# A graph layer with residual and layer norm: another warm-up operand, eight banks for the weight preparation, and its transposes put into two groups

## The chip, the cores and the metric

The kernel runs on one core of a Trainium2 chip. The metric is the device time of one execution in microseconds. PE is TensorE (PEld its weight loads), DVE is VectorE, ACT is ScalarE, POOL is GpSimd, SP is SyncE. PSUM has eight banks of 128 partitions by 512 fp32 columns; PE writes its results there.

## The reference

The input is x (32 batches, 256 nodes, 512 features), an adjacency of 256 by 256, four weights of 512 by 512 and two scalars. Cut to what matters:

```python
z_l = h @ W_lang.T;  z_g = h @ W_grav.T;  v = h @ W_V.T
zn  = z_l / max(norm(z_l), EPS)
A_l = max(zn @ zn.T, 0) * not_eye
d2  = max(sq + sq.T - 2 * z_g @ z_g.T, 0)
A_g = exp(-d2 / (2 * sigma**2)) * not_eye
K   = w_l * row_stochastic(A_l * adj) + (1 - w_l) * row_stochastic(A_g * adj)
x   = layernorm(x + (K @ v) @ W_O.T)
```

## The kernel before

Every fp32 matrix is split into a high and a low part in PE's rounded fp32 format, and a product is the sum of three (high by high, high by low, low by high).

**Preparation.** Before the first batch the kernel works out the two symmetric matrices M = W.T W of W_lang (called L) and W_grav (called G), and the product of W_V and W_O. The work is a list, `prep_units`, of 22 units, run by PE in the order of the list. Each unit fills one PSUM bank, and ACT and then DVE copy it out as its high and its low part:

- UPPER (g, i): one row of blocks of M, 12 products. For i = 0 they are 512 columns wide, for i = 1 to 3 they are 256 wide (the function `row_blocks`; the other blocks of the row come by symmetry).
- MIRROR (g, i): two transposes of 128 by 128 out of `m_hi`, the blocks that symmetry gives; ACT alone copies them out and counts them in `mirrored`. They read the rows that `made(r, i)` names.
- WO_TURN (i): four transposes of W_O, which lies in the tile `y`.
- WVO (i): 12 products of 512 columns, W_V by the turned W_O. The first waits until POOL has made the low part of W_V (`v_split`) and DVE that of the last WO_TURN.

The order before is UPPER L 0 to 3, UPPER G 0, then for i = 1, 2, 3: MIRROR L i, WO_TURN i-1 (with WO_TURN 3 in the last round), UPPER G i; then MIRROR G 1, WVO 0, MIRROR G 2, WVO 1, MIRROR G 3, WVO 2, WVO 3. Unit u goes to bank u % 4 and waits (`emptied`) until unit u - 4 has been copied out. Each MIRROR waits for ACT's copy of the last UPPER row of its matrix (`prepared(UPPER, g, DT - 1)`).

ACT runs `prep_hi_part(u)` and DVE `prep_lo_part(u)` in the order of the units. Between them stand other pieces of work at fixed units: on ACT the casts of W_V (`value_weight_hi`) and, at the units `SPLIT_AT` (WVO 0 and WVO 1), the high parts of the first two batches (`turn_hi`); on DVE their 32 by 32 block transposes (`turn`), their low parts (`turn_lo`), the `diagonals`, `scales` and `scaled_rest` of M. POOL makes the low part of W_V, then the triangles that give `md_hi`, ending in `m_ready[g]`.

**Before the preparation** PE runs `WARM` = 9 products of zeros. DVE clears a tile of 512 columns (`kt_hi` of batch 0) for them. PE then needs `ident_ready`, which POOL gives, and then starts with UPPER L 0 (`first_block`), whose parts it waits for one 128-row block at a time (`w_hi_ready`, `w_lo_ready`).

**The body.** Batches are taken in 16 pairs: pairs 0, 1 and 14 are written out, twelve are in a hardware loop, and the last has an order of its own. A pair has eight projections (`project`, four for L and then four for G), four tiles of values, four tiles of x M x.T, and the four products K by v of the pair before. Projection k goes to bank (22 + k) % 4; in pair 0 the first four wait with `emptied(PREP - 4 + k)`, later ones for `proj_ready`. Banks 4 and 5 take the x tiles, banks 6 and 7 the products with v.

## Time and profile before

| | |
|---|---|
| Time, median of 3 runs | 650.01 us (648.86 to 652.34) |
| Time of the profiled execution | 648.58 us |
| Its span in the trace | 646.8 us |
| PE busy | 638.5 us, 2861 products and transposes |
| DVE, ACT, POOL busy | 534.9, 384.1, 136.5 us |

A busy time is the sum over one engine's instructions. Products are pipelined, so the printed length of one is longer than the distance to the next: what a product costs in a stream is the distance from one start to the next. Times in rows count from the start of the span.

### The profile page before, as it was taken

To read this page: it belongs to the slowest core of one execution; us is meant where nothing else is said; L and a number is where in the kernel's file an instruction comes from. 1 tells how busy PE (TensorE), PEld (TensorE's weight loads), DVE (VectorE), ACT (ScalarE), POOL (GpSimd) and SP (SyncE) were. 2 spreads that over 40 slices of the span, in tenths; PEclk is the share of its full clock that TensorE was granted. 3 is DMA by queue.
4 is the path that set the end of the run, shared out by engine and by line. 5 is a ranking of instruction groups with operands and counts; after the bars stand their busy time and mean duration, and the time that the engine had idled before them with its cause. 6 is when DMAs were issued, how large, how long until landed. Compare 5 with 4: busy or idle time off the path is not lost.

```text
span 646.8 us, 10734 instructions
## 1 busy us (share of the span) xinstructions
PE 638.5 (99%) x2861; PEld 529.2 (82%) x2861; DVE 534.9 (83%) x1431; ACT 384.1 (59%) x709; POOL 136.5 (21%) x287
## 2 busy tenths in 40 slices
PE   9999999999999999999999999999999999999996
PEld 7888888888888888888888888888888888888884
DVE  6874979798897978889797988879788887978786
ACT  5544545656565565656556575655657565565775
POOL 3612011211221121122112112221211222121132
PEclk9999999999999999999999999999999999999999
DMA  9321757483765748385574938657492865546353
GB/s 299 80 62 61 187 142 165 133 244 96 216 161 171 199 128 249 94 245 143 160 198 138 250 83 242 148 163 193 141 250 79 253 141 161 160 151 192 100 184 123
DMA packets 141509, 106.48 MB, mean 165 GB/s; under 512 B 40112, under 2 KB 115632, under 8 KB 141488
## 3 DMA queue, kind: packets, MB, share of 16 engines
q1 hardware_dynamic: 140768, 104.40, 57.9%
q0 software_dynamic: 288, 1.05, 0.5%
q10 hardware_dynamic: 432, 0.79, 0.3%
q8 instruction: 9, 0.15, 0.1%
q14 instruction: 12, 0.10, 0.0%
HBM read 65.80 MB, written 40.40 MB: 164 GB/s over the span
## 4 chain that ended last, share of the span: by engine, by line
PE 98%; ACT 0%; DVE 0%; issue 0%; POOL 0%; POOLq 0%
PE bank L1425 62%; PE bank L1515 18%; PE bank L1520 15%; PE bank L1472 2%; PE bank L1493 1%; PE bank L1561 0%; PE bank L1482 0%; PE bank L1477 0%; ACT y L821 0%; PE bank L1448 0%; PE bank L1451 0%; PE bank L1452 0%; POOL last_rstd L680 0%; DVE xq L1322 0%; DVE m_lo L1316 0%
## 5 line engine op out<-in xcount | busy, mean ns | idle before, releaser
L761 ACT ACTIVATE p_hi<-bank,m_scale 128x512 fp32r<-128x512 f32 x128 | 86.2, 684 | 54.9 <-PE bank L1520 53.8
L1061 DVE SCALAR_TENSOR_TENSOR p_lo<-bank,m_scale,p_hi 128x512 fp32r<-128x512 f32 x128 | 94.2, 747 | 19.0 <-ACT p_hi L761 18.9
L1520 PE MATMUL bank<-hT_lo,m_hi 128*128 128x512 f32 x384 | 107.8, 389 | 0.0
L1425 PE MATMUL bank<-wvo_hi,hT_hi 128*128 128x512 f32 x256 | 99.8, 390 | 0.0
L1425 PE MATMUL bank<-wvo_hi,hT_lo 128*128 128x512 f32 x256 | 99.6, 389 | 0.0
L1425 PE MATMUL bank<-wvo_lo,hT_hi 128*128 128x512 f32 x256 | 99.6, 389 | 0.0
L1425 PE MATMUL bank<-p_hi,hT_hi 128*128 128x512 f32 x256 | 99.6, 389 | 0.0
L1425 PE MATMUL bank<-p_lo,hT_hi 128*128 128x512 f32 x256 | 99.6, 389 | 0.0
L1520 PEld LDWEIGHTS bank<-hT_lo,m_hi 128*128 128x128 f32 x384 | 72.1, 188 | 15.0
L628 POOL TENSOR_TENSOR rnorm<-norm,minus_half 128x2 f32<-128x2 f32 x32 | 34.8, 1088 | 231.0 <-DVE norm L1089 231.0
L1515 PE MATMUL bank<-hT_hi,m_lo 128*128 128x512 f32 x192 | 69.5, 389 | 0.0
L765 ACT CAST v_hi<-bank 128x512 fp32r<-128x512 f32 x60 | 32.4, 589 | 62.5 <-PE bank L1425 62.5
L776 ACT COPY xs<-bank 128x512 f32<-128x512 f32 x64 | 37.2, 581 | 47.2 <-PE bank L1425 47.2
L1515 PE MATMUL bank<-hT_hi,m_hi 128*128 128x512 f32 x192 | 64.3, 389 | 0.0
L1425 PEld LDWEIGHTS bank<-wvo_hi,hT_lo 128*128 128x128 f32 x256 | 48.0, 188 | 10.0
L1425 PEld LDWEIGHTS bank<-p_lo,hT_hi 128*128 128x128 f32 x256 | 48.1, 188 | 10.0
L1425 PEld LDWEIGHTS bank<-p_hi,hT_hi 128*128 128x128 f32 x256 | 48.0, 188 | 10.0
L1425 PEld LDWEIGHTS bank<-wvo_lo,hT_hi 128*128 128x128 f32 x256 | 48.1, 188 | 9.9
L1425 PEld LDWEIGHTS bank<-wvo_hi,hT_hi 128*128 128x128 f32 x256 | 48.0, 188 | 9.9
L1515 PE MATMUL bank<-hT_hi,md_hi 128*128 128x512 f32 x128 | 49.8, 389 | 0.0
L1176 DVE SCALAR_TENSOR_TENSOR work<-work,coef 128x256 f32<-128x256 f32 x60 | 26.5, 483 | 25.6 <-ACT work L795 25.6
L1425 PE MATMUL bank<-v_hi,kt_hi 128*128 128x512 f32 x120 | 46.9, 391 | 0.0
(164 smaller groups left out, 1266.7 us busy)
## 6 DMA issues: line engine op xcount, KB each, us to landing
x_blk<-in_x SPq DMA_DIRECT2D x128, 128.0 KB, 3.4
x_spill<-xs SPq DMA_DIRECT2D x30, 512.0 KB, 3.8
xq<-x_spill SPq DMA_DIRECT2D x120, 128.0 KB, 3.4
x_nat<-in_x SPq DMA_DIRECT2D x30, 512.0 KB, 4.0
out_y<-y SPq DMA_DIRECT2D x30, 512.0 KB, 3.4
k_spill<-work SPq DMA_DIRECT2D x30, 256.0 KB, 2.2
work<-k_spill SPq DMA_DIRECT2D x120, 64.0 KB, 2.2
r_row<-r_spill SPq DMA_DIRECT2D x32, 128.0 KB, 3.5
```

Of the source, the lines that this page charges most:

```text
L628: nc.gpsimd.tensor_tensor(rnorm[:, b, 0:NT], norm2[:, b], minus_half[:], ALU.pow).then_inc(pool_steps, 1)
L761: nc.scalar.activation(p_hi[:, :, j, g, :], src[:].rearrange("p (b n) -> p b n", b=2), ACT.Copy, scale=m_scale[:, g, j:j + 1]).then_inc(pr ...
L765: nc.scalar.copy(last_v(m_hi, b, t) if is_last(p) else v_hi[:, b, t], src[:]).then_inc(proj_hi, 1)
L776: nc.scalar.copy(dst, src).then_inc(x_saved, 1)
L1061: nc.vector.scalar_tensor_tensor(out=p_lo[:, :, j, g, :], in0=src[:].rearrange("p (b n) -> p b n", b=2), scalar=m_scale[:, g, j:j + 1], in ...
L1176: nc.vector.scalar_tensor_tensor(out=wk_row(b, KER, t), in0=wk_row(b, KER, t), scalar=coef[:, b, L, t:t + 1], in1=wk_row(b, GAUSS, t), op0 ...
L1425: last = pe.matmul(dst, lhsT, rhs, start=(n == 0), stop=(n == len(steps) - 1))
L1472: last = pe.matmul(row_blocks(dst[:], i), lhsT, rhs, start=(n == 0), stop=(n == len(steps) - 1))
L1493: pe.matmul(kv_bank[1][:], kt_hi[:, 0, 0, 0], in_kt(kt_hi, 0), start=True, stop=True)
L1515: pe.matmul(pbank(k)[:], stationary, hi[i], start=(i == 0), stop=False)
L1520: last = pe.matmul(pbank(k)[:], md_hi[:, g, 0] if i == 0 else m_hi[:, g, i, c], lo[i], start=False, stop=(i == DT - 1))
```

## The change

Three things are edited.

- The zeros for the first products: POOL clears 128 columns of `kt_hi` as its first instruction, ahead of `ident`, where DVE cleared 512 columns. Each product reads the 128 columns four times as its moving operand (a pattern with stride 0), and is still 512 columns wide. There are eight products in place of nine.
- The banks: unit u goes to bank u % 8 and waits for unit u - 8. The first four projections wait for the last unit that used their bank (`last_unit_in`).
- The order: MIRROR L 1 to 3 and WO_TURN 0 to 3 stand together behind UPPER G 0; UPPER G 1 to 3 and WVO 0 follow; MIRROR G 3, 1, 2 stand together behind WVO 0; WVO 1 to 3 end the list. A MIRROR waits for the rows that it reads and no longer for the last row. The first projection of each matrix waits for the latest of its mirrors (`mirrors_of`).

```diff
--- before.py
+++ after.py
@@ -230,6 +230,7 @@
 
 
         bank = [ctx.enter_context(nc.psum_tensor(f"bank{i}", [P, WIDE], F32)) for i in range(8)]
+        prep_bank = bank
         proj_bank = bank[0:4]
         x_bank = bank[4:6]
         kv_bank = bank[6:8]
@@ -329,15 +330,11 @@
 
         UPPER, MIRROR, WO_TURN, WVO = range(4)
 
+
         prep_units = [(UPPER, L, i) for i in range(DT)] + [(UPPER, G, 0)]
-        for i in range(1, DT):
-            prep_units += [(MIRROR, L, i), (WO_TURN, None, i - 1)]
-            if i == DT - 1:
-                prep_units += [(WO_TURN, None, i)]
-            prep_units += [(UPPER, G, i)]
-        for i in range(1, DT):
-            prep_units += [(MIRROR, G, i), (WVO, None, i - 1)]
-        prep_units += [(WVO, None, DT - 1)]
+        prep_units += [(MIRROR, L, i) for i in range(1, DT)] + [(WO_TURN, None, k) for k in range(DT)]
+        prep_units += [(UPPER, G, i) for i in range(1, DT)] + [(WVO, None, 0)]
+        prep_units += [(MIRROR, G, i) for i in (3, 1, 2)] + [(WVO, None, i) for i in range(1, DT)]
         PREP = len(prep_units)
 
 
@@ -359,9 +356,9 @@
 
             return sum(kind == MIRROR for kind, _, _ in prep_units[:u + 1])
 
-        def mirror_of(g, i):
-
-            return mirrors_upto(prep_units.index((MIRROR, g, i)))
+        def mirrors_of(g):
+
+            return max(mirrors_upto(prep_units.index((MIRROR, g, i))) for i in range(1, DT))
 
         def live(p):
 
@@ -382,6 +379,10 @@
         def pbank(k):
 
             return proj_bank[(PREP + k) % 4]
+
+        def last_unit_in(k):
+
+            return max(u for u in range(PREP) if prep_bank[u % 8] is pbank(k))
 
         def in_order(cols):
 
@@ -394,7 +395,7 @@
         PV = 2 * DT + 2 * NT
         BLKS = 16 * (P // BLK)
         LOOPS = (PAIRS - 4) // 2
-        WARM = 9
+        WARM = 8
 
 
         def load_quarter(queue, k):
@@ -560,6 +561,7 @@
         @block.gpsimd
         def _(pool):
 
+            nc.gpsimd.memset(kt_hi[:, 0, 0, 0].bitcast(F32), 0.0).then_inc(warm_ready, 1)
             nc.gpsimd.memset(ident[:], 0.0).then_inc(zeroed, 1)
             pool.wait_ge(zeroed, 1)
             nc.gpsimd.affine_select(out=ident[:], in_=ident[:], compare_op=ALU.not_equal, fill=1.0, base=0,
@@ -713,7 +715,7 @@
             def prep_hi_part(u):
 
                 kind, g, i = prep_units[u]
-                src = proj_bank[u % 4]
+                src = prep_bank[u % 8]
                 act.wait_ge(prep_done, u + 1)
                 if kind == MIRROR:
                     if i == 2:
@@ -941,8 +943,6 @@
 
         @block.vector
         def _(dve):
-            nc.vector.memset(in_kt(kt_hi, 0).bitcast(F32), 0.0).then_inc(warm_ready, 1)
-
             def turn(p, b):
 
                 if not live(p):
@@ -971,7 +971,7 @@
             def prep_lo_part(u):
 
                 kind, g, i = prep_units[u]
-                src = proj_bank[u % 4]
+                src = prep_bank[u % 8]
                 if kind == MIRROR:
                     return
                 dve.wait_ge(prep_hi, upto_unit(u))
@@ -1454,10 +1454,10 @@
 
             def prepare(u):
                 kind, g, i = prep_units[u]
-                dst = proj_bank[u % 4]
+                dst = prep_bank[u % 8]
                 rows = slice(i * P, (i + 1) * P)
-                if u >= 4:
-                    emptied(u - 4)
+                if u >= 8:
+                    emptied(u - 8)
                 if (kind, g, i) == (UPPER, L, 0):
                     last = first_block(dst)
                 elif kind == UPPER:
@@ -1472,8 +1472,9 @@
                         last = pe.matmul(row_blocks(dst[:], i), lhsT, rhs, start=(n == 0), stop=(n == len(steps) - 1))
                 elif kind == MIRROR:
 
-                    pe.wait_ge(prep_hi, prepared(UPPER, g, DT - 1))
-                    for r in [r for r in range(DT) if made(r, i)]:
+                    sources = [r for r in range(DT) if made(r, i)]
+                    pe.wait_ge(prep_hi, prepared(UPPER, g, max(sources)))
+                    for r in sources:
                         last = pe.transpose(dst[:, r * P:(r + 1) * P], m_hi[:, g, r, rows].bitcast(F32), ident[:])
                 elif kind == WO_TURN:
                     for b in range(2):
@@ -1489,8 +1490,10 @@
 
 
             pe.wait_ge(warm_ready, 1)
+            zeros = kt_hi[:, 0, 0, 0]
             for n in range(WARM):
-                pe.matmul(kv_bank[1][:], kt_hi[:, 0, 0, 0], in_kt(kt_hi, 0), start=True, stop=True)
+                pe.matmul(kv_bank[1][:].rearrange("p (r c) -> p r c", c=P), zeros, zeros.unsqueeze(1).broadcast_to([P, DT, P]),
+                          start=True, stop=True)
             pe.wait_ge(ident_ready, 1)
             for u in range(PREP):
                 prepare(u)
@@ -1502,11 +1505,11 @@
                     pe.wait_ge(hT_hi_ready, upto(p, 2, 2))
                 if type(p) is int and p == 0 and j == 0:
                     pe.wait_ge(m_ready[g], 1)
-                    pe.wait_ge(mirrored, mirror_of(g, DT - 1))
+                    pe.wait_ge(mirrored, mirrors_of(g))
                 if not (type(p) is int and p == 0 and k < 4):
                     pe.wait_ge(proj_ready, upto(p, PV, k - 3))
                 else:
-                    emptied(PREP - 4 + k)
+                    emptied(last_unit_in(k))
                 hi = [hT_hi[parity][:, i].rearrange("p b n -> p (b n)") for i in range(DT)]
                 lo = [hT_lo[parity][:, i].rearrange("p b n -> p (b n)") for i in range(DT)]
                 c = slice(j * P, (j + 1) * P)
```

## Rows read from the trace of the kernel before

**Rows 1.** The page: busy time of the engines, and the chain's shares by engine.

```profile
PE 638.5 (99%) x2861; PEld 529.2 (82%) x2861; DVE 534.9 (83%) x1431; ACT 384.1 (59%) x709; POOL 136.5 (21%) x287
...
PE 98%; ACT 0%; DVE 0%; issue 0%; POOL 0%; POOLq 0%
```

**Rows 2.** Windows: stretch and length, busy us (x instructions) by engine, clock, DMA.

```profile
15.87:35.11 19.24, 18.69 (x113) 16.34 (x112) 16.91 (x43) 10.21 (x23) 11.54 (x13) 1.00 0.41 94
...
35.11:637.00 601.89, 601.89 (x2668) 498.19 (x2667) 502.88 (x1343) 360.81 (x662) 117.26 (x249) 1.00 0.59 163
```

**Rows 3.** Waits of PE over the span: us in total, times, longest.

```profile
PE bank L1477 <- ACT m_hi L728: 0.6, 1, 0.6
```

**Rows 4.** Timeline from 0 to 8 us: start, us, engine, line, operation.

```profile
0.82 0.20 POOL L563 MEMSET ident<- 128x128 f32 x1 [0.29 <-POOLq L1676]
...
1.00 0.48 DVE L944 MEMSET kt_hi<- 128x512 f32 x1 [1.00 <-PEq L1676]
...
1.54 4.21 PE L1493 MATMUL bank<-kt_hi 128*128 128x512 f32 x9 [1.54 <-DVE kt_hi L944]
...
3.96 1.14 ACT L706 CAST p_hi<-xs 128x512 fp32r<-128x512 f32 x2 [0.93 <-DMA xs<-in_L_gnn_W_lang]
4.61 2.67 DVE L967 TENSOR_TENSOR p_lo<-xs,p_hi 128x512 fp32r<-128x512 f32 x4 [3.13 <-ACT p_hi L706]
...
5.55 1.05 PE L1448 MATMUL bank<-p_hi 128*128 128x512 f32 x2
...
6.40 0.52 PE L1451 MATMUL bank<-p_lo,p_hi 128*128 128x512 f32 x1
...
6.75 0.40 PE L1452 MATMUL bank<-p_hi,p_lo 128*128 128x512 f32 x1
```

**Rows 5.** Timeline from 8 to 16 us: the first product of the second unit.

```profile
8.81 0.28 PE L1472 MATMUL bank<-p_hi 128*128 128x256 f32 x1
```

**Rows 6.** Timeline of PE from 20 to 24.2 us.

```profile
20.34 1.04 PE L1482 MATMUL bank<-ident,y 128*128 128x128 f32 x8
21.21 0.39 PE L1472 MATMUL bank<-p_hi 128*128 128x256 f32 x1
21.43 0.28 PE L1472 MATMUL bank<-p_lo,p_hi 128*128 128x256 f32 x1
...
22.62 0.28 PE L1472 MATMUL bank<-p_hi,p_lo 128*128 128x256 f32 x1
23.45 0.41 PE L1477 MATMUL bank<-ident,m_hi 128*128 128x128 f32 x2 [0.55 <-ACT m_hi L728]
```

**Rows 7.** Timeline of PE from 34.8 to 41.8 us.

```profile
34.89 0.39 PE L1425 MATMUL bank<-hT_hi,v_lo 128*128 128x512 f32 x1
35.11 0.39 PE L1515 MATMUL bank<-hT_hi,md_hi 128*128 128x512 f32 x1
...
41.69 0.39 PE L1515 MATMUL bank<-hT_hi,md_hi 128*128 128x512 f32 x1
```

**Rows 8.** Timeline of ACT from 15.7 to 39 us.

```profile
16.56 0.38 ACT L724 CAST m_hi<-bank 128x256 fp32r<-128x256 f32 x1
16.82 0.61 ACT L731 CAST hT_hi<-bank 128x512 fp32r<-128x512 f32 x1
17.30 1.16 ACT L711 CAST v_hi<-xq 128x512 fp32r<-128x512 f32 x2
...
22.94 0.37 ACT L728 CAST m_hi<-bank 128x256 fp32r<-128x256 f32 x1 [0.88 <-PE bank L1472]
```

**Rows 9.** Timeline of DVE from 15.7 to 39 us.

```profile
23.34 0.42 DVE L979 TENSOR_TENSOR m_lo<-bank,m_hi 128x256 fp32r<-128x256 f32 x1
...
33.41 1.21 DVE L961 TENSOR_TENSOR hT_lo<-hT_raw,hT_hi 128x1024 fp32r<-128x1024 f32 x1
```

**Rows 10.** Timeline of POOL from 15 to 41 us.

```profile
18.02 2.53 POOL L586 TENSOR_TENSOR v_lo<-xq,v_hi 128x512 fp32r<-128x512 f32 x2 [1.09 <-ACT v_hi L711]
...
38.67 1.29 POOL L606 TENSOR_TENSOR md_hi<-md_hi,junk_a 128x512 fp32r<-128x512 f32 x1
```

## Prediction, made before the changed kernel had run

> **What bounds the kernel now.** I read the page first, then the waits of PE, then the timeline of the stretch that the diff touches. The page says that PE is busy for 638.5 us of a span of 646.8, and holds 98% of the chain that ended last [rows 1]. So a microsecond counts only if it is one in which PE starts later, idles, or does work that it need not do. The second view is the windows: from 35.11 us, where the first projection starts, to 637 us PE is busy for the whole 601.89 us [rows 2]. Nothing in the body waits for anything but PE, and the body is not edited. If PE reaches the first projection d us earlier, the end comes d us earlier, as long as no other engine is late for the body's first waits. The third view is the waits: past the start, the only one of PE that is printed is that of the transposes of line 1477 for ACT's copy `m_hi`, 0.6 us [rows 3]. Everything that this change can move therefore lies before 35.11 us, in three places: the start, that wait, and small losses at bank waits.
>
> **Prices of PE's work.** Starts, not lengths, give the price. A product of 256 columns costs 0.12 us (ten of them from 21.43 to 22.62), and a transpose 0.109 us (eight from 20.34 to 21.21) [rows 6]. A product of 512 columns costs 0.227 us (29 of them from 35.11 to 41.69) [rows 7]. At the start it is different: the two products from 5.55 to 6.40 make 0.427 us each, the nine zero products from 1.54 to 5.55 the same with 0.17 for the first weight load, and from 6.75 the nine up to 8.81 make 0.23 [rows 4, 5]. These are TensorE's two levels, 1.2 and 2.4 GHz; the engine rose to the upper one at about 6.6 us, some 5.1 us after its first product. The profile's granted clock is at full speed for this stretch too, so there I go by the distances.
>
> **The start.** What releases PE is the clearing on DVE, which starts at 1.00 and takes 0.48; PE starts 0.06 after it [rows 4]. POOL's first clearing of 128 columns started at 0.82 and took 0.20 [rows 4]. The new clearing stands in its place, so it ends at 1.02 and PE starts at 1.08, 0.46 earlier. Eight products then end at 1.08 + 0.17 + 8 x 0.427 = 4.66, where nine ended at 5.55. The real work needs ACT's first cast, which starts at 3.96; DVE, which waits for it, starts at 4.61 [rows 4], and so could PE. So the first real product can stream from 4.79 (the cast, plus 0.17 for a first weight load). It gains 0.76, but the data are now near: the second cast ends at 5.10, and DVE's four low parts end from 5.28 to 7.28 [rows 4]. At 0.427 a product PE needs 1.28 us for three, and ACT and DVE deliver a block about each 0.7, so after a bubble of 0.1 at the second product PE is the slower one. If the clock rises at the same moment as before (6.65), four products are done by then and eight more at 0.227 end the block at 8.43; before, the next unit started at 8.81 [rows 5]: 0.38 gained. If the rise moves with PE's start (6.19), the block ends at 8.23: 0.58 gained. The rise cannot be worked out from one trace; I take 0.45. Bounds: if the clock were high from the start, the last low part (7.28) and two products end it near 7.8, 1.0 gained; if it stayed low for all twelve products, 4.79 + 12 x 0.427 = 9.91, 1.1 lost.
>
> The Trainium skill (TensorE: Matmul & The Clock Gate, section "What's actually happening") says that the chip's watch on the engine does not restart with the kernel, and that the point of the rise varies by about 500 ns from run to run. By that page the 0.38 and not the 0.58 would be the mean, with a scatter of some tenths; the single trace here can't show it.
>
> The pattern with stride 0 is not in the trace. Nearest are the products of the second unit, which read two strided blocks of 128 columns (the row at 8.81 [rows 5]) and take the same time as the plain 256 of UPPER G 3 [rows 6]. From below it costs nothing; from above each re-read stops the stream and the eight products take twice as long, so that the first real one comes near 8.1 and the block ends at 8.1 + 2.72 = 10.8, 2.0 lost. I take nothing, as the rows of strided blocks are the nearest. POOL's `ident` and constants move back by 0.13 to 0.2; PE asks for `ident` only after the zero products, and DVE first in the diagonals behind UPPER L 0, later than 8.81. DVE loses an instruction at a time when it idles until 4.61 [rows 4].
>
> **The stretch from UPPER G's first row to the first projection.** It is 19.24 us long, from 15.87 to 35.11 [rows 2]. Its work is 28 transposes (12 of M, 16 of W_O), 36 products of 256 columns and 48 of 512: 28 x 0.109 + 36 x 0.12 + 48 x 0.2267 = 3.05 + 4.32 + 10.88 = 18.25. So 0.98 us are not work. The largest piece is seen: the last 256-column product starts at 22.62 and the transpose behind it at 23.45, which is 0.83 where 0.12 is due [rows 6]: 0.71 lost, because MIRROR G 1 waits for ACT's copy of UPPER G 3, which starts at 22.94 and takes 0.37 [rows 8]. The rest, 0.27, is in small pieces: a bank wait of UPPER G 3 for the unit four before (21.21 to 21.43 is 0.22 where 0.12 is due [rows 6]), the like at UPPER G 2, and what is left over, which I put down to the three changes from transposes to 512-column products, some 0.03 each.
>
> In the new order WVO 0, 12 x 0.2267 = 2.72 us of work, stands between UPPER G 3 and MIRROR G. The copy that took PE's 0.71 now lies beneath it: cover 2.72, need about 0.8. With eight banks the bank waits are for units at least eight back, which are copied long before. Two of three changes from transpose to product go. Gained: 0.98 - 0.03 = 0.95. The work itself stays the same: grouping removes no instruction, and a switch between transposes and products of 256 costs nothing that I can find.
>
> **What could be late instead.** Let PE reach 15.88 - 0.4 = 15.48 (0.4 of the 0.45 above). ACT must now copy three mirrors, four turned W_O and two casts of W_V with no product of PE between. At the distances between its starts (0.26 for a mirror, 0.48 for a bank, and 1.16 for two casts [rows 8]) it is done with WO_TURN 3 near 20.0, and DVE near 21.0. PE leaves the transposes at 15.48 + 22 x 0.109 = 17.88 and wants WO_TURN 3 only for WVO 0, at 17.88 + 4.32 = 22.2: slack 1.2. POOL's last low parts of W_V ran from 18.02 for 2.53 [rows 10] and start some 0.2 later now, done near 20.8: slack 1.4. ACT copies UPPER G 1 and 2 late, behind WO_TURN, but MIRROR G asks at 24.9.
>
> The tightest is DVE. The low part of UPPER G 3 starts at 23.34 and that of the second batch at 33.41, for 1.21, ending at 34.62 [rows 9]; the fifth product of the first projection waits for it. PE now comes to that product at 35.11 - 1.4 + 0.91 = 34.6. UPPER G 3 ends on PE at 22.2 and not at 22.74, and its low part starts near 22.8, so the chain moves up by about 0.5 and ends near 34.1: slack 0.5. If it did not move at all, the wait would be under 0.1. And `m_ready[G]`, needed by projection 4: POOL's last add starts at 38.67 and takes 1.29 [rows 10], so 39.96 even unmoved, and PE asks at 41.69 - 1.4 = 40.3 [rows 7].
>
> **Sum.** 0.45 + 0.95 = 1.40 us. The profiled execution took 648.58 and would take 647.2; its span would be 645.4. The median of the runs shown, 650.01, lies 1.43 above the profiled one, and I subtract from it: 648.6.
>
> **The rivals.**
>
> 1. *A new wait takes part of the gain.* DVE's chain to the second batch's low part stays where it is or slips (a block of W_O copied while POOL works, DVE's longer instructions beside POOL), or ACT's nine copies in a row hold WVO 0. For it: slack of 0.5 at the tightest. Against: DVE's first step comes earlier. A slip of 1 us leaves 0.9 gained: 649.1.
> 2. *The start gives nothing.* The stride-0 read is slower, or the clock rises later since the engine has a small gap after its zeros. At the low level for all twelve products 1.1 is lost against 0.95: 650.2; with every re-read stopping the stream 2.0 is lost: 651.1.
> 3. *Slower than before: the clock falls.* The place is behind the 22 transposes in a row, 2.4 us, where before there were at most ten, 1.09 us, the last eight of them from 20.34 to 21.21, after which products still ran at the upper level [rows 6]. If the engine fell there and needed as long to rise as at the start, 5.1 us, it would lose 5.1 x (1 - 0.227 / 0.427) = 2.4 us: 650.01 + 2.4 - 1.4 = 651.0. It decides once the low stretch is longer than 1.4 / 0.47 = 3.0 us; to be slower by over 0.5% it would have to be over 9.9 us. The Trainium skill (TensorE: Matmul & The Clock Gate, section "Part 4: PE-mode transpose") says that transposes don't count as activity of the engine in the way that products do; by that rule this is where it would bite. The ten transposes of this trace don't bear it out.
> 4. *The start gives more*: the rise falls early in the block, 1.0 and not 0.45 gained, 648.1.
>
> **How the numbers follow.** Forecast with its own range of 648.1 to 649.0: 0.62. Rival 1: 0.15. Rival 2: 0.09. Rival 3: 0.06. Rival 4: 0.08. A measurement of this kernel tells about 0.5% (3.25 us) from no change, and every case here is below it: even the best gives 1.95 us and the worst costs 1.0. Faster by over 0.5% would need the runs themselves to scatter (they span 3.5 us around 650): 0.10. Slower by over 0.5% needs rival 3 with a long low stretch, or scatter: 0.03. Within: 0.87. The scatter is larger than the terms, so the range is 647.0 to 650.7: from the forecast down by 1.6 for a median that falls at the fast end of the runs, and up past rival 1 and the first of rival 2's figures, short of rival 3.
>
> **What the profile after would show.** PE's first zero product at about 1.1 and the first real one at 4.8; the second UPPER unit at 8.2 to 8.5; no gap before the transposes of line 1477; PE's waits left with the start alone; the first projection at 33.7 and the last product some 1.4 earlier. I am wrong if the zero products stand more than 0.43 apart, if products behind the long group of transposes stand 0.43 apart, or if the fifth product of the first projection waits for DVE.

## The result, and the profile after

| | before | after |
|---|---|---|
| Median of 10 runs | 648.91 us (648.47 to 652.34) | 647.24 us (646.98 to 647.62) |
| Mean of the ten | 649.72 us | 647.25 us |
| Profiled execution (span) | 648.58 us (646.8) | 647.46 us (645.7) |

The ratio is 0.9967, with a 95% interval of 0.9953 to 0.9981: 0.33% faster, and clear of no change. Two things besides the medians count below. The ten runs of the kernel before spread over 3.9 us, those of the changed one over 0.6; so the means lie 2.5 us apart and the medians 1.7. Much of that is two runs of the kernel before, at 652.15 and 652.34: without them its mean is 649.09, and the means lie 1.8 us apart.

The page of the changed kernel, engines and counts (one product and one weight load fewer, one clearing moved from DVE to POOL, against [rows 1]):

```profile
PE 638.4 (99%) x2860; PEld 529.1 (82%) x2860; DVE 535.9 (83%) x1430; ACT 383.7 (59%) x709; POOL 136.6 (21%) x288
```

Its windows, for the preparation from the first transpose on and for the body, with the columns of [rows 2]:

```profile
15.71:34.02 18.31, 18.31 (x114) 16.33 (x112) 17.43 (x46) 9.91 (x23) 11.88 (x14) 1.00 0.48 105
34.02:636.00 601.98, 601.98 (x2668) 498.37 (x2667) 504.72 (x1344) 360.88 (x662) 117.25 (x249) 1.00 0.59 163
```

The preparation takes 18.31 us where it took 19.24, and PE is busy for all of it; the body is as long as it was and as full. The only wait of PE left in the view of waits is the start:

```profile
PE bank L1495 <- POOL kt_hi L564: 1.1, 1, 1.1
```

The timeline of PE at the start (start, us, engine, line, operation), which answers to [rows 4] and [rows 5]:

```profile
1.07 3.78 PE L1495 MATMUL bank<-kt_hi 128*128 128x512 f32 x8 [1.07 <-POOL kt_hi L564]
4.70 1.22 PE L1448 MATMUL bank<-p_hi 128*128 128x512 f32 x2
...
6.57 0.62 PE L1448 MATMUL bank<-p_hi 128*128 128x512 f32 x1
7.00 0.44 PE L1451 MATMUL bank<-p_lo,p_hi 128*128 128x512 f32 x1
7.28 0.39 PE L1452 MATMUL bank<-p_hi,p_lo 128*128 128x512 f32 x1
...
8.66 0.28 PE L1472 MATMUL bank<-p_hi 128*128 128x256 f32 x1
```

PE starts 0.47 earlier and its first real product 0.85 earlier than before. But 6.57 to 7.00 is still 0.43 a product and 7.00 to 7.28 is 0.28: here the engine rose to its upper level at about 7.0 us, where it was 6.6 before, and the second unit starts at 8.66 and not between 8.2 and 8.5. From there the same timeline shows the 22 transposes in a row, the place where the gap of 0.83 was [rows 6], and the first projection:

```profile
15.72 0.82 PE L1478 MATMUL bank<-ident,m_hi 128*128 128x128 f32 x6
16.37 1.91 PE L1483 MATMUL bank<-ident,y 128*128 128x128 f32 x16
18.03 0.36 PE L1472 MATMUL bank<-p_hi 128*128 128x256 f32 x1
...
22.30 0.28 PE L1472 MATMUL bank<-p_hi,p_lo 128*128 128x256 f32 x1
22.42 0.40 PE L1425 MATMUL bank<-hT_hi,v_hi 128*128 128x512 f32 x1
25.18 0.82 PE L1478 MATMUL bank<-ident,m_hi 128*128 128x128 f32 x6
...
34.02 0.39 PE L1518 MATMUL bank<-hT_hi,md_hi 128*128 128x512 f32 x1
...
34.92 0.39 PE L1523 MATMUL bank<-hT_lo,md_hi 128*128 128x512 f32 x1
```

22.30 to 22.42 is 0.12 and nothing is idle. WVO 0 runs from 22.42 to 25.18, and ACT's copy of UPPER G 3, the one PE waited for before [rows 8], lies beneath it:

```profile
22.62 0.37 ACT L730 CAST m_hi<-bank 128x256 fp32r<-128x256 f32 x1 [1.07 <-PE bank L1472]
```

The last thing to see is on DVE and POOL, and the prediction only touched on it. A *diagonal* is the DVE operation that multiplies a block of M by `ident` and sums it; there are two for each row of blocks, one of `m_hi` and one of `m_lo`. Timeline of DVE, its `diagonals` of UPPER L 3 (first two) and the first of UPPER G 0; then POOL in the same stretch:

```profile
14.70 1.25 DVE L991 CUSTOM_DVE_ANT_0 x_nat<-m_hi,ident 128x128 f32<-128x128 f32 x1
15.89 1.36 DVE L991 CUSTOM_DVE_ANT_0 x_nat<-m_lo,ident 128x128 f32<-128x128 f32 x1
...
17.89 0.29 DVE L991 CUSTOM_DVE_ANT_0 x_nat<-m_hi,ident 128x128 f32<-128x128 f32 x1
```

```profile
14.52 2.58 POOL L588 TENSOR_TENSOR v_lo<-xq,v_hi 128x512 fp32r<-128x512 f32 x2 [6.71 <-ACT v_hi L713]
```

The same instruction on the same shape takes 0.29 in one place and 1.25 and 1.36 in another: the long ones stand beside POOL's two subtractions (14.52 to 17.10), the short one in the pause behind them. Here nobody waits for them.

### The profile page after: what moved, and what is told of

Read it like the earlier page. It is cut to its first block, busy times and chain, and to the rows that moved or that the text cites. A ratio compares the mean times of both kernels' runs of the same rounds, so it can differ in the third digit from the quotient of the medians.

```text
span 645.7 us, 10728 instructions
## 1 busy us (share of the span) xinstructions
PE 638.4 (99%) x2860; PEld 529.1 (82%) x2860; DVE 535.9 (83%) x1430; ACT 383.7 (59%) x709; POOL 136.6 (21%) x288
## 4 chain that ended last, share of the span: by engine, by line
PE 98%; ACT 0%; DVE 0%; POOL 0%; issue 0%; POOLq 0%
PE bank L1425 62%; PE bank L1518 18%; PE bank L1523 15%; PE bank L1472 2%; PE bank L1495 1%; PE bank L1483 0%; PE bank L1564 0%; PE bank L1448 0%; ACT y L823 0%; PE bank L1478 0%; PE bank L1451 0%; PE bank L1452 0%; POOL last_rstd L682 0%; DVE xq L1322 0%; DVE m_lo L1316 0%
## 5 line engine op out<-in xcount | busy, mean ns | idle before, releaser
L630 POOL TENSOR_TENSOR rnorm<-norm,minus_half 128x2 f32<-128x2 f32 x32 | 34.8, 1088 | 230.0 <-DVE norm L1089 230.0
```

The lines of the kernel that those rows point to most:

```text
L630: nc.gpsimd.tensor_tensor(rnorm[:, b, 0:NT], norm2[:, b], minus_half[:], ALU.pow).then_inc(pool_steps, 1)
```

## The experiments

Each time is a median (lowest to highest, number of runs), each ratio is to the kernel before on the same chip. The diffs are cut to the lines that matter. The first theory, A, was that of the prediction: the start gives some tenths, the preparation gives 0.95. Its rival, B, said that the start gives 0.7 or more in most executions, because the clock rises earlier. A third, C, stands in the expectation of the second experiment: in some executions of the kernel before PE has a further wait. In the later expectations, on the zero products, the letter A has the meaning that they give it.

**The start alone**, the list and the four banks as before:

```diff
-            nc.vector.memset(in_kt(kt_hi, 0).bitcast(F32), 0.0).then_inc(warm_ready, 1)
+            nc.gpsimd.memset(kt_hi[:, 0, 0, 0].bitcast(F32), 0.0).then_inc(warm_ready, 1)
-        WARM = 9
+        WARM = 8
```

with the changed kernel's zero products.

> The eight zero products on POOL's 128 columns, on the preparation of the kernel before. Theory A (the preparation gives 0.95 us of the 1.1 by which the profiled spans differ, and the start what is left): first product at 1.07 us, first projection 0.1 to 0.6 earlier than the 35.11 of before, so at 34.5 to 35.0, the gap of 0.83 before the transposes still there; median 0.2 to 0.6 below before. Theory B (the medians differ by 1.67, so the start is worth 0.7 or more in most executions, by an earlier rise of the clock): median 0.7 to 1.2 below before.

Measured: 648.35 us (647.8 to 650.8, 12), ratio 1.0002 (0.999 to 1.0014). Neither the gain of theory A nor that of B is there, and three of twelve runs lie above 650.5. The profiled one, 650.8, is of these. PE, timeline:

```profile
18.02 0.60 PE L1481 MATMUL bank<-ident,y 128*128 128x128 f32 x4
20.78 0.38 PE L1471 MATMUL bank<-p_hi 128*128 128x256 f32 x1 [2.16 <-DVE hT_lo L982]
```

It waits 2.16 us, ahead of UPPER G 2, whose bank WO_TURN 0 has filled, for DVE's low part of that bank. DVE's timeline says why that is late:

```profile
14.62 1.16 DVE L990 CUSTOM_DVE_ANT_0 x_nat<-m_hi,ident 128x128 f32<-128x128 f32 x1
15.71 1.36 DVE L990 CUSTOM_DVE_ANT_0 x_nat<-m_lo,ident 128x128 f32<-128x128 f32 x1
...
17.73 1.12 DVE L990 CUSTOM_DVE_ANT_0 x_nat<-m_hi,ident 128x128 f32<-128x128 f32 x1
18.78 1.34 DVE L990 CUSTOM_DVE_ANT_0 x_nat<-m_lo,ident 128x128 f32<-128x128 f32 x1
20.05 0.68 DVE L982 TENSOR_TENSOR hT_lo<-bank,hT_hi 128x512 fp32r<-128x512 f32 x1
```

The four diagonals take 5.0 us where 1.2 would do, and stand ahead of the copy. POOL worked from 14.35 to 16.93 and from 17.43 to 19.97. The same view of the kernel before:

```profile
14.19 0.29 DVE L991 CUSTOM_DVE_ANT_0 x_nat<-m_hi,ident 128x128 f32<-128x128 f32 x1
14.41 1.38 DVE L991 CUSTOM_DVE_ANT_0 x_nat<-m_lo,ident 128x128 f32<-128x128 f32 x1
...
17.64 0.29 DVE L991 CUSTOM_DVE_ANT_0 x_nat<-m_lo,ident 128x128 f32<-128x128 f32 x1
```

There DVE was done with the second pair at 17.93, and POOL's second turn began at 18.02 [rows 10]: 0.1 us apart. This gave theory C its cause: *a diagonal that starts while POOL subtracts ends only with POOL's operation; whether that happens hangs on tenths of a microsecond; and in a ring of four banks PE then waits.*

**The preparation alone** (banks and order), with the old start and nine products:

> The eight banks and the new order, with DVE's clearing and nine zero products of before. Both theories: the stretch from the first transpose to the first projection falls from 19.24 to 18.3 us. Theory A: median 0.9 to 1.0 below before. Theory B: the same 0.9 to 1.0, and the rest of the 1.67 is in the start. Theory C (the preparation is worth more than its stretch, because a wait of PE in it costs some executions more): median 1.3 or more below before, and no executions far above the median.

Measured: 647.44 us (646.81 to 647.99, 12), ratio 0.9981 (0.9973 to 0.999). Its windows:

```profile
15.99:34.30 18.31, 18.31 (x114) 16.33 (x112) 17.09 (x44) 9.91 (x23) 11.56 (x13) 1.00 0.43 98
```

18.31 again, PE without a wait but the start, and no run above 648.0. The median lies 1.06 below the kernel before, near theory A's figure and short of the 1.3 of theory C, whose narrow spread is there: 1.2 us, where 30 runs of the kernel before on this chip spread over 3.1. The preparation carries most of the result, and the narrower spread.

**The eight banks alone**, order and start as before:

```diff
-                dst = proj_bank[u % 4]
+                dst = prep_bank[u % 8]
-                if u >= 4:
-                    emptied(u - 4)
+                if u >= 8:
+                    emptied(u - 8)
...
```

ACT and DVE read the same banks, and the first projections wait for `last_unit_in`.

> Eight banks with the order and the start of before. Theory: the bank waits at UPPER G 2 and 3 (0.07 and 0.08) go, but then MIRROR G 1 is reached 0.15 earlier and waits 0.15 longer unless ACT's copy of UPPER G 3 comes earlier too, which it does, as PE makes that unit earlier: gap before MIRROR G 1 stays 0.83, stretch 19.24 to 19.1. Rival: the eight banks are what removes the gap: stretch 18.4 or less.

Measured: 648.08 us (647.68 to 649.28, 12), ratio 0.9988 (0.9978 to 0.9999). The stretch is 19.13 us and not 19.24, and the gap ahead of MIRROR G 1 is the old 0.83. No run lies above 650; but of the 30 runs of the kernel before on this chip only two did, so twelve runs alone say little on that.

**The order alone**, in four banks, with the old start:

```diff
-        prep_bank = bank
+        prep_bank = bank[0:4]
```

and every `u % 8`, `u - 8` made `u % 4`, `u - 4`.

> The new order on four banks, with the start of before. Theory: WO_TURN 0 now stands directly behind three mirrors and waits for DVE's low part of UPPER G 0 (ends about 1.7 us after PE gets there), and each next turn for a copy four units back, so PE loses 1 to 2 us before UPPER G 1 and gains 0.8 at MIRROR G: first projection at 35.0 to 36.0, median within 1 us of before. Rival (the order alone carries the gain): first projection at 34.2, median 0.9 below before.

Measured: 651.42 us (650.4 to 652.89, 7), ratio 1.0045 (1.0029 to 1.006). PE's waits:

```profile
PE bank L1426 <- DVE wvo_lo L984: 1.8, 1, 1.8
PE bank L1484 <- DVE m_lo L980: 0.7, 1, 0.7
```

So the new order needs the banks: alone it makes the kernel slower by 2.9 us. The expectation was too low: the first projection came at 38.0 us where 35 to 36 had been expected, and the median was to be within 1 us of before.

**The start with the diagonals moved.** To take the wait of the first experiment away, the pairs of UPPER L 3 and UPPER G 0 were put behind the low part of UPPER G 2:

```diff
-                if kind == UPPER and (g == L or i in (0, 2)):
+                if kind == UPPER and g == L and i < DT - 1:
                     diagonals(g, i)
+                if (kind, g, i) == (UPPER, G, 2):
+                    diagonals(L, DT - 1)
+                    diagonals(G, 0)
+                    diagonals(G, 2)
```

> e1_start_only with DVE's diagonals of L's last row and G's first moved behind UPPER G 2, so that DVE copies the turned W_O first. Theory C (the executions far above the median are DVE's diagonals beside POOL's low part of W_V, which hold the banks of the four-bank ring): no execution more than 1 us above the lowest, PE's wait of 2.2 us before UPPER G 2 gone, median 0.5 or more below that of e1_start_only. Rival (late loads or a late rise of the clock make them): a third of the executions still 1.5 to 3 us above the lowest.

Measured: 650.86 us (649.32 to 651.29, 7), ratio 1.003 (1.0018 to 1.0041). The expectation failed. The wait before UPPER G 2 is gone, but three pairs of diagonals now stand ahead of W_O's last low part, and PE's timeline has the wait later:

```profile
24.37 0.47 PE L1428 MATMUL bank<-hT_hi,v_hi 128*128 128x512 f32 x1 [1.33 <-DVE hT_lo L982]
```

Four of the seven runs had a mean granted clock of 0.995 over the span and took 650.86 to 651.29, the others 0.997 or 0.998 and at most 649.9. Two more executions of this kernel (649.71 and 649.97 us) were profiled to find one of the former, and both had 0.998, with the same two waits of PE (0.6 and 1.3 us) and no slow products behind them in the preparation. So what makes the runs at 0.995 is not known from here.

> The kernel of e5_start_diagonals_later once more. If the profiled execution has a clock of 0.995 and a span near 649: theory (the clock falls behind PE's two gaps before WVO 0, 0.83 and 1.6 us): products of WVO 0 or 1 stand 0.43 apart for some 3.4 us, 1.6 us lost. Rival (late rise): the first block ends at 9.5 or later and nothing behind it is slow.

> The same as e13_look_one, for a second chance that the profile falls on an execution with the clock of 0.995; the same two readings.

**The start and the eight banks**, with the order as before:

> e1_start_only with eight banks and the order of before. Theory C: DVE's diagonals may still take over 1 us, but no unit waits for them, so no execution is more than 1 us above the lowest; the gap of 0.83 before MIRROR G 1 stays, and the median lies 0.7 to 0.9 above that of the changed kernel, near 648.0. Rival: the tail of e1_start_only (four of twelve 1.3 to 2.5 above its median) stays.

Measured: 648.24 us (647.84 to 649.17, 11), ratio 0.9992 (0.9983 to 1.0001). No run lies above 650, as the start alone had three above 650.5 (on another chip); the runs spread over 1.3 us where at most 1 was expected, and of the start's gain the median shows nothing. The profiled one had both pairs drawn out as in the first experiment (the last at 18.71, for 1.36), and PE didn't wait before UPPER G 2. But the expectation that no unit waits for them failed: the lateness reaches PE further on, before WVO 0, for less:

```profile
24.25 0.47 PE L1429 MATMUL bank<-hT_hi,v_hi 128*128 128x512 f32 x1 [0.85 <-DVE hT_lo L987]
```

**The start without POOL's subtraction.** The low part of W_V is cleared in place of being worked out, on the old order and four banks; what it is read for afterwards is left out of the computation with it:

```diff
-                nc.gpsimd.tensor_tensor(by_feature(w_parts[2][1][:, k]), in_order(raw[2][:, k]),
-                                        by_feature(w_parts[2][0][:, k]).bitcast(F32),
-                                        ALU.subtract).then_inc(v_split, 1)
+                nc.gpsimd.memset(w_parts[2][1][:, k].bitcast(F32), 0.0).then_inc(v_split, 1)
```

> e1_start_only with POOL's four subtractions that give the low part of W_V replaced by clearings, so W_V's low part is left out of the result. Theory C: every diagonal of DVE takes 0.29, DVE's low part of the turned W_O is in time, PE does not wait before UPPER G 2, and the executions lie within 1 us, near 647.9. Rival (loads or the clock make the tail of e1_start_only, 650.6 to 650.8 in three of twelve): the tail stays with a diagonal of 0.29.

Measured: 647.85 us (647.63 to 649.06, 12), ratio 0.9985 (0.9974 to 0.9997). DVE, then PE, on the timeline:

```profile
16.69 0.29 DVE L988 CUSTOM_DVE_ANT_0 x_nat<-m_hi,ident 128x128 f32<-128x128 f32 x1
16.91 0.29 DVE L988 CUSTOM_DVE_ANT_0 x_nat<-m_lo,ident 128x128 f32<-128x128 f32 x1
```

```profile
17.46 0.60 PE L1479 MATMUL bank<-ident,y 128*128 128x128 f32 x4
17.86 0.39 PE L1469 MATMUL bank<-p_hi 128*128 128x256 f32 x1
```

POOL, in the same stretch:

```profile
14.66 1.04 POOL L587 MEMSET v_lo<- 128x512 f32 x2 [6.75 <-ACT v_hi L710]
17.27 1.04 POOL L587 MEMSET v_lo<- 128x512 f32 x2 [1.57 <-ACT v_hi L710]
```

All diagonals up to there take 0.29, UPPER G 2 stands right behind the transposes, no run is above 649.1 (they spread over 1.4 us, 1 was expected), and the median is 0.92 us under the kernel before. So without the subtraction the upper tail is gone and the gain of the start is there. The profile itself is no test of the collision: its diagonals ended at 14.13 and 17.20, before each of POOL's turns, and none stood beside a clearing. Nor does it set aside the rival of its expectation, that the loads make the tail. ACT's first cast of W_grav, which waits for a load, started at 7.44 here and at 8.44 in the profile of the start alone; over all eighteen profiles it started between 7.23 and 8.51. With casts at 7.50 and 7.29, and the subtraction in place, the pair of UPPER L 3 came as early (13.68 and 13.47, in two experiments further down, the zeros from a constant and the transposes made four times) and was as short. The two may well belong together: a later load brings DVE to the pair when POOL has begun, and POOL's subtraction then draws it out. No run changes the load by itself.

That a diagonal is drawn out by the subtraction is shown by the rows of all profiles: each one that started while POOL subtracted ended about 0.15 us after POOL's operation, whether that took 0.35 or 1.43 us in all. The Trainium skill (SBUF — State Buffer, section "SBUF: two separate sides") says that DVE and GpSimd share one pair of ports as an exclusive lock for the length of an instruction, and that on DVE's side an operation with two SBUF inputs asks for it only against a GpSimd operation that reads SBUF. The trace agrees on the lock: the diagonal reads `m_hi` or `m_lo` and `ident`, all in SBUF, and is drawn out beside a subtraction, while DVE's low parts, which read one input from PSUM, take 0.67 to 0.69 beside it and away from it. That an operation of POOL that only writes leaves the diagonal alone, no run here shows.

**POOL's subtraction done twice**, in the kernel before and in the changed one (the second waits for the first; the result is the same):

```diff
+                nc.gpsimd.tensor_tensor(by_feature(w_parts[2][1][:, k]), in_order(raw[2][:, k]),
+                                        by_feature(w_parts[2][0][:, k]).bitcast(F32),
+                                        ALU.subtract).then_inc(extra, 1)
+                pool.wait_ge(extra, k + 1)
```

> The kernel before with POOL's four subtractions for W_V's low part made twice; the result is the same. POOL's work then lasts to about 25 us. Theory C: DVE's diagonals of G's first row fall beside it and take over 1 us, PE waits about 2 us before UPPER G 2 as in e1_start_only, then 0.83 before MIRROR G 1 and some before WVO 0: span 2 to 4 us above before. If the clock falls in such waits, products behind them stand 0.43 apart and 1.6 more is lost. Rival: PE waits only for W_V's low part itself, 1.3 us, and the clock stays.

Measured: 650.93 us (650.4 to 651.27, 8), ratio 1.0022 (1.0005 to 1.0039). PE's waits:

```profile
PE bank L1477 <- DVE hT_lo L988: 1.1, 1, 1.1
PE bank L1430 <- DVE hT_lo L988: 0.7, 1, 0.7
PE bank L1482 <- ACT m_hi L733: 0.6, 1, 0.6
```

This is the test of the collision: the second pair, 0.29 each in the kernel before, now falls into POOL's work and takes 0.58 and 1.35:

```profile
17.51 1.35 DVE L996 CUSTOM_DVE_ANT_0 x_nat<-m_lo,ident 128x128 f32<-128x128 f32 x1
```

So the old start too gets the wait before UPPER G 2 when POOL works through DVE's second pair; it is 1.1 us, where about 2 was expected.

> The same doubling in the changed kernel. DVE's diagonals are drawn out too, but no bank is waited for; PE waits once, before WVO 0 (22.2 to 22.5 us), until POOL is done at about 25.0: 2.5 us, span 2.5 above the changed kernel. If the clock falls in a wait of that length, products of WVO 0 stand 0.43 apart and 1.6 more is lost; rival: it stays and WVO 0 runs at 0.227.

Measured: 652.06 us (650.51 to 653.52, 8), ratio 1.0049 (1.0029 to 1.0069): slower than the old kernel with the same burden. In the changed kernel everything that is late gathers at one place, WVO 0. PE, timeline, and two windows:

```profile
21.65 0.28 PE L1477 MATMUL bank<-p_hi,p_lo 128*128 128x256 f32 x1
25.41 0.77 PE L1430 MATMUL bank<-hT_hi,v_hi 128*128 128x512 f32 x1 [3.48 <-issue]
...
30.25 0.63 PE L1430 MATMUL bank<-hT_hi,v_lo 128*128 128x512 f32 x1
```

```profile
25.40:30.60 5.20, 5.19 (x12) 4.02 (x13) 4.93 (x9) 1.04 (x1) 4.77 (x8) 0.50 0.35 101
31.60:40.00 8.40, 8.40 (x39) 6.97 (x38) 8.15 (x19) 2.91 (x7) 1.62 (x2) 1.00 0.22 63
```

The row of 25.41 names nobody for the wait. DVE's last low part of W_O ended at 21.26, and POOL's last subtraction at 25.31, so it was POOL:

```profile
24.04 1.27 POOL L593 TENSOR_TENSOR v_lo<-xq,v_hi 128x512 fp32r<-128x512 f32 x1
```

The wait was 3.5 us (2.5 expected), and behind it the granted clock is 0.50, the lower level, for 5.2 us in which twelve products take 0.43 each. At 0.227 they would take 2.7. So the gap costs 3.5 + 2.5, and the transposes behind WVO 0 a few tenths more. The eight runs' mean clocks sort with their times: 0.997 at 650.51, 0.994 or 0.995 from 651.7 to 652.4, 0.993 above 653.3.

**The transposes of W_O four times**, 70 in a row in place of 22, for the prediction's rival 3:

```diff
-                    for r in range(DT):
+                    for r in list(range(DT)) * 4:
```

> The changed kernel with each transpose of W_O made four times, so that 70 transposes stand in a row, 7.6 us; nothing of the result changes. Theory (transposes hold the clock): the added 48 cost 0.109 each, 5.2 us, and the products of UPPER G 1 behind them stand 0.12 apart; median 5.2 above the changed kernel. Rival 3 of the prediction (the clock falls in a run of transposes): products behind them stand 0.21 to 0.43 apart for some us, and the median is 6.5 or more above.

Measured: 652.14 us (652.01 to 652.22, 4), ratio 1.0052 (1.0037 to 1.0068), 4.9 above the changed kernel's 647.24. PE, timeline:

```profile
15.74 7.15 PE L1483 MATMUL bank<-ident,y 128*128 128x128 f32 x64
22.64 0.36 PE L1472 MATMUL bank<-p_hi 128*128 128x256 f32 x1
22.85 0.28 PE L1472 MATMUL bank<-p_lo,p_hi 128*128 128x256 f32 x1
22.96 0.28 PE L1472 MATMUL bank<-p_hi,p_lo 128*128 128x256 f32 x1
```

64 transposes take 6.9 us, 0.108 each, and the products behind them stand 0.12 apart: the upper level throughout. 48 x 0.108 = 5.2 is the whole cost. Rival 3 falls: three times the length of the group shows no fall. The rule of the Trainium skill (TensorE: Matmul & The Clock Gate, section "Part 4: PE-mode transpose"), that transposes don't count as activity as products do, is not borne out by this run.

**Four zero products**, and the changed kernel a second time on the same chip:

```diff
-        WARM = 8
+        WARM = 4
```

> The changed kernel with four zero products, so that PE idles from 2.95 to about 4.7 us. Theory (the rise needs PE to be busy before it): the rise comes up to some us later, the first block ends at 9 to 10 us in place of 8.67, median 0.5 to 1.7 above the changed kernel. Rival (the zeros are worth nothing, ACT's first cast bounds the start and the rise comes with the real products as early): median within 0.2 of it.

> The changed kernel on the same chip and in the same rounds as the others of this call. Median 0.9 to 1.7 below the kernel before, executions within 0.7 us of each other, as before.

Measured: 648.39 us (647.91 to 649.15, 12), ratio 0.9994 (0.9981 to 1.0006), against 647.30 us (646.73 to 648.23, 12), ratio 0.9968 (0.9952 to 0.9984). The real products start at 4.76 after four zeros and at 4.98 after eight. But after four the engine idles for 1.6 us before them and stays at 0.43 a product to about 8.0; the first block ends at 9.18, and at 8.50 after eight. The eight products are worth 1.1 us between the medians. The changed kernel's twelve runs spread over 1.5 us, where at most 0.7 had been expected from the 0.6 of the first ten. In its second profile the diagonals of UPPER L 3 and UPPER G 0 take 0.29 and the stretch is again without a wait: two patterns on DVE, one time on PE.

**Zeros from a constant**, so that PE waits for nobody, on two chips:

```diff
-            pe.wait_ge(warm_ready, 1)
-            zeros = kt_hi[:, 0, 0, 0]
+            zeros = nc.const_aps.tensor(0.0, (P, 1), F32).bitcast(F32R)
             for n in range(WARM):
...
+                pe.matmul(kv_bank[1][:], zeros.broadcast_to([P, P]), zeros.broadcast_to([P, WIDE]), start=True, stop=True)
```

> The changed kernel with its zero products reading one column of the constant 0.0, which is written before the kernel's first instruction, so that PE waits for no clearing: first product at 0.8 to 0.9 us in place of 1.07. Theory A (the start is bounded by ACT's first cast and by the moment of the clock's rise, which does not move with PE's start): first real product still at 4.70, median within 0.15 of the changed kernel. Rival (the rise follows PE's first product): median 0.1 to 0.3 lower.

> e8_constant_zeros beside the changed kernel. Theory A: within 0.15 of e11_changed_again. Rival (PE's earlier start moves the rise): 0.2 to 0.4 below it.

Measured: 646.92 us (646.78 to 647.35, 8), ratio 0.9973 (0.9963 to 0.9984), and 646.91 us (646.76 to 647.5, 12), ratio 0.9969 (0.9957 to 0.9982). PE, in the second:

```profile
0.86 3.75 PE L1492 MATMUL bank<-const-float32-0.0 128*128 128x512 f32 x8 [0.86 <-PEq L1675]
4.78 0.93 PE L1446 MATMUL bank<-p_hi 128*128 128x512 f32 x2 [0.17 <-ACT p_hi L706]
```

The products start 0.2 earlier; the first real one stays where ACT's cast puts it. Beside the changed kernel on one chip the medians differ by 0.4 and the means by 0.3, about two standard errors. That is the rival's figure of 0.2 to 0.4 and not theory A's 0.15, but not far enough from either to decide: perhaps a little faster, and at least as good. It is the fastest version run here.

## Why the prediction was right and where it was wrong

**The preparation** went as worked out: 0.93 gained where 0.95 was forecast, the gap of 0.83 gone, the copy hidden beneath WVO 0. No wait came in its place; the slack at the fifth product of the first projection was 0.3 (DVE's low part of the second batch ran from 33.39 to 34.6, PE came at 34.92), not 0.5.

**The start** was built rightly: first product at 1.07 (forecast 1.08), first real one at 4.70 (4.79), stride 0 at no cost, since the eight products stand 0.43 apart like the plain ones. The term of 0.45 cannot be checked on one pair of profiles, in which it measures 0.15. The clock's rise differs from execution to execution. The second unit began at 8.81, 8.93, 9.14, 9.20 and 8.40 in the five profiles with the old start, mean 8.90, and from 7.93 to 8.66 in the ten with the new one and its eight products, mean 8.25. That is 0.65 gained on the average. The prediction argued in one place that 0.38 would be the mean and not 0.58; the fifteen profiles speak for the 0.58, a rise that comes earlier by as much as PE's start.

**What the body and the rivals did.** The body didn't change. Rival 1's collision, DVE's longer instructions beside POOL, is real: it stands in the profile after, at 14.70 and 15.89. But in the changed kernel it is covered: UPPER G 1 to 3, 4.3 us of products, stand between the last transpose and WVO 0, and no bank is asked for again before it is eight units old. Rival 2's price was not paid. Rival 3 is false at three times the length. Rival 4, a better start with 1.0, is further from the average of 0.65 than my own term of 0.45.

**The step that failed** is in "How the numbers follow": "A measurement of this kernel tells about 0.5% (3.25 us) from no change, and every case here is below it", and "The scatter is larger than the terms". I took the 3.5 us over which the runs of the kernel before spread for something a measurement adds to any kernel. The runs showed something else: ten of each kernel gave an interval of 0.9953 to 0.9981, which is 0.14% or 0.9 us either way, and the change, 1.67 us between the medians or 0.33%, is clear of it. The base of the sum was wrong with it: 650.01 is a median of three runs, one of them at 652.34, and the ten have 648.91. From there the sum of 1.4 would have given 647.5, where 647.24 was measured. That 647.24 still lies in the range is owed to the 1.6 us by which I had widened it downwards for the scatter, and not to the forecast of 648.6.

A term was left out too, for I priced the change on one profiled execution. It was one in which DVE's second pair of diagonals missed POOL by 0.1 us. The term is what PE loses in the old ring of four banks when they meet: nothing in that execution and 2.16 us in the one profiled with the new start. The difference of the medians doesn't need it (0.93 for the preparation and 0.65 for the start make 1.58). It bears on the spread:

- The start alone shows no gain (1.0002, interval 0.999 to 1.0014) although PE's second unit begins earlier. In the one execution profiled, among its slowest, the gain goes back at UPPER G 2; for the others that is a conclusion. Without POOL's subtraction the start brings 0.92.
- The list and banks together cut off the top of the spread: the highest of twelve is 647.99, where 30 runs of the kernel before on the same chip reached 650.74. Eight banks alone reached 649.28; the start with eight banks still waits 0.85 before WVO 0 in its profile.
- With the subtraction doubled, the old start and the old ring lose 1.1 at that place as well.

The changed kernel's runs span 0.6 us in the first ten and 1.5 in twelve more, and not 3.9.

**What stays open.** No execution of the kernel before at the upper end of its spread was profiled. That it waits at UPPER G 2 in them is concluded from the kernel with the new start and from the one with the subtraction doubled. The start alone, the start with eight banks and the start without the subtraction were run on three chips, and tails of three in twelve against none in eleven or twelve are few runs to go by. The slowest executions of the kernel before, four of the 100 beside the experiments, at 652.0 to 652.4, also had a mean clock of 0.995, and so one more stretch at the lower level than the rest; no clock is on record for the two at 652.15 and 652.34 among the first ten, but they stand at the same height. The fall is shown only in the changed kernel with a gap of 3.5 us, and which gap sets it off in the old kernel is not known. So how much of the spread of 3.9 us is the wait and how much the clock is open.

## What to carry to other kernels

When the runs of a kernel spread and PE is its bound, look in several profiles for a wait that is there in some of them: a change that covers it may gain more than one trace can show, and a change upstream of it can lose its gain there. Take the base of a forecast from enough runs that one slow one doesn't move it. Give a ring of buffers the depth that the worst execution needs, and not the one at hand; but see that reordering doesn't gather all lateness ahead of one unit, where one long gap costs the clock as well. Before placing a DVE operation with two SBUF inputs, see what POOL reads at that time.

## What the runs showed of the hardware

- A DVE operation of 0.29 us on two SBUF tiles took 0.35 to 1.43 when it started while POOL subtracted two SBUF tiles: as long as POOL's operation still lasted, and about 0.15 more. DVE's copies with one input in PSUM kept their 0.67 to 0.69.
- One gap of 3.5 us on PE was followed by 5.2 us at the lower level; behind the 2.16 us gap of the start alone the next product came at the usual distances.
- With the same instructions ahead of it the second unit began between 7.93 and 8.66 us in ten profiled executions, because the clock rose at different times.
- 70 transposes in a row, 7.6 us, kept the upper level: the products behind them stood 0.12 us apart.
